# First products of experts 1 to 7 as seven products of quarters, and one buffer for each of the two weights

## The reference

```
tokens = x_flat[index].reshape(E, expert_capacity, hidden)
inter = jax.nn.relu(jnp.einsum('ech,eih->eci', tokens, first_linear))
out = jnp.einsum('eci,ehi->ech', inter, second_linear)
out = out * vals[:, :, None]
final = jnp.zeros((n_tokens, hidden), x.dtype).at[index].add(out.reshape(-1, hidden))
```

## Time and profile before

| what | before |
|---|---|
| median of three runs | 1437.44 us |
| the profiled execution itself | 1439.36 us |
| its span, first to last instruction | 1437.6 us |
| TensorE busy | 1320.3 us (92%) |
| VectorE busy | 952.7 us (66%) |
| ScalarE busy | 805.5 us (56%) |
| GpSimd busy | 739.0 us (51%) |
| TensorE in the two products, lines 1196 and 1210, share of the chain that ended last | 23% each |

### The profile page before, as it was taken

The page is one execution under the profiler, slowest core; times in us unless marked ns, Lnnn a source line. Parts: engine busy times, 40 slices in busy tenths (PEclk is TensorE's granted clock), DMA queues, the critical chain, the costliest instruction groups (busy, mean ns, idle before and its releaser), DMA issues.

```text
span 1437.6 us, 30587 instructions
## 1 busy us (share of the span) xinstructions
PE 1320.3 (92%) x12330; PEld 780.1 (54%) x12330; DVE 952.7 (66%) x1808; ACT 805.5 (56%) x1272; POOL 739.0 (51%) x781
## 2 busy tenths in 40 slices
PE   7649999989998999997849999999999999999996
PEld 3436777767676777774527444444444444444442
DVE  8768898979889787888775545454454545455421
ACT  4658888868998899987354514233241514334210
POOL 3458878877888778887323332242514224251301
PEclk9959999989999899999969999999999999999998
DMA  6157998968887786888433564565646555654401
GB/s 197 54 117 179 221 237 210 236 175 184 210 222 167 180 175 181 184 221 210 125 115 103 164 183 141 154 177 138 157 125 180 144 151 166 156 140 125 103 16 43
DMA packets 319574, 228.88 MB, mean 159 GB/s; under 512 B 253305, under 2 KB 253689, under 8 KB 319434
## 3 DMA queue, kind: packets, MB, share of 16 engines
q1 hardware_dynamic: 304074, 176.28, 49.4%
q0 software_dynamic: 15360, 50.66, 12.1%
HBM read 118.98 MB, written 50.86 MB: 118 GB/s over the span
## 4 chain that ended last, share of the span: by engine, by line
PE 74%; DVE 10%; POOL 8%; issue 3%; ACT 2%; SPq 1%; DMA 1%; DVEq 0%; POOLq 0%; ACTq 0%
PE ps L1210 23%; PE ps L1196 23%; PE ps L1096 9%; PE ps L1026 7%; PE ps L1077 3%; PE ps L1113 2%; POOL sd L547 2%; PE ps L1010 2%; DVE sm L1461 1%; PE ps L1049 1%; POOL qT L527 1%; DVE x L1483 1%; POOL ph L553 1%; PE ps L999 1%; POOL oT L533 1%
## 5 line engine op out<-in xcount | busy, mean ns | idle before, releaser
L1196 PE MATMUL ps<-xT,w1s 128*128 128x512 f16 (+1 forms) x1632 | 336.3, 368 | 1.9 <-DVE xT L1726 1.5
L1210 PE MATMUL ps<-w2s,hT 128*128 128x512 f16 x1536 | 332.8, 379 | 0.0
L848 ACT ACTIVATE hT<-ps 128x512 f16<-128x512 f32 (+1 forms) x136 | 77.5, 572 | 356.3 <-PE ps L1196 292.5
L1196 PEld LDWEIGHTS ps<-xT,w1s 128*128 128x128 f16 x1632 | 160.7, 99 | 175.3 <-issue 1.9
L1210 PEld LDWEIGHTS ps<-w2s,hT 128*128 128x128 f16 x1536 | 150.3, 98 | 181.2
L598 POOL DMA_INDIRECT out_dram<-ys,idx x64 | 71.8, 1121 | 278.0 <-DVE ys L1766 278.0
L1026 PE MATMUL ps<-xnT,wqh 128*128 128x256 f16 x1536 | 198.3, 281 | 8.2 <-ACT partq L736 8.1
L1096 PE MATMUL ps<-woh,oT 128*128 128x512 f16 x768 | 182.2, 386 | 5.4 <-POOL oT L533 5.2
L1756 DVE SCALAR_TENSOR_TENSOR hT<-ps,hT 128x512 f16<-128x512 f32 (+1 forms) x136 | 88.4, 658 | 140.4 <-ACT hT L848 88.7
L1766 DVE SCALAR_TENSOR_TENSOR ys<-ps,gs,og 128x512 f32<-128x512 f32 x64 | 48.1, 751 | 189.4 <-PE ps L1210 189.4
L553 POOL TENSOR_TENSOR ph<-sd,ph 128x1232 f16<-128x1232 f32 x64 | 162.2, 2535 | 18.7 <-ACT ph L759 18.0
(11 more groups left out here) (206 smaller groups left out, 2013.0 us busy)
## 6 DMA issues: line engine op xcount, KB each, us to landing
xr<-x SPq DMA_DIRECT2D x64, 256.0 KB, 3.4
xrow_dram<-x SPq DMA_DIRECT2D x64, 256.0 KB, 3.6
out_dram<-x SPq DMA_DIRECT2D x64, 256.0 KB, 4.0
stage<-w1T SPq DMA_DIRECT2D x8, 2048.0 KB
stage<-w2T SPq DMA_DIRECT2D x8, 2048.0 KB, 8.4
xt<-x SPq DMA_DIRECT2D x59, 256.0 KB, 3.2
xs<-x SPq DMA_DIRECT2D x56, 256.0 KB, 4.1
wqf<-wq SPq DMA_DIRECT2D x1, 1024.0 KB, 7.2
```

What stands on the lines that cost most here:

```text
L1196: ins = pe.matmul(hb[z][:, 0:wide], w1s[e % 2][:, a, k, ic * P:(ic + 1) * P], xT[:, 4 * b + k, cols], start=(k == 0 and i == 0), stop=(k = ...
L1210: ins = pe.matmul(yb[z][:, :], hT[:, a, k, s * P:(s + 1) * P], w2s[e % 2][:, b, k, :], start=(k == 0 and i == 0), stop=(k == 7 and i == 2))
```

## The change

Expert 0 stays as it was. For experts 1 to 7 the first product, a 1024 by 512 matrix of weights times 512 by 1024 of rows, is cut into four quarters on each side. By Strassen's scheme (in the form with shared sums) the four quarters of the result come from seven products of quarters (sums and differences of them) instead of eight. A quarter's product is four tiles (j = 0 to 3) of 128 by 512, each over 2 chunks in 3 passes, so 6 matmuls; 28 such tiles are 168 matmuls.

The order of the 28 tiles is the table `PRODUCTS`, pairs of product p and tile j. Products 1, 6, 7 and 4 of one j follow each other in one PSUM bank (`hb[j % 2]`); in between ScalarE copies what stands there to `running` (`part_out`), since each intermediate sum is also the start of one quarter of the result. Product 2 has bank 2, products 5 and 3 share bank 3. VectorE adds bank 2 or 3 to the copy (`sum_up`), then ScalarE makes the high part (`sum_hi`) and VectorE the low one (`sum_lo`). TensorE waits for these by the semaphores `part` and `sum`.

The sums of quarters are made by GpSimd in place: four of 128x256 for each pair of row tiles p and p + 4 (`row_sums`), four of 128x1024 for the weights (`weight_sums`). They lie between the gathers and the scatters. The split and the transpose have then 12 chunks of original rows (`raw_hi`, `raw_lo`, `raw_T`) and 16 chunks of sums (`sums_hi`, `sums_lo`, `sums_T`) for each p, and the weights have seven quarters to convert instead of four pieces of the same 1024 columns (`left_hi`, `left_lo`). `w1s` and `w2s` have one buffer each, `og` has four places instead of eight. Lines are left out where marked.

```diff
+PRODUCTS = ((1, 0), (2, 0), (5, 0), (6, 0), (1, 1), (7, 0),
+            (2, 1), (6, 1), (3, 0), (4, 0), (5, 1), (7, 1),
+            (1, 2), (2, 2), (3, 1), (6, 2), (4, 1), (5, 2), (7, 2),
+            (1, 3), (2, 3), (3, 2), (6, 3), (4, 2), (7, 3), (5, 3), (4, 3), (3, 3))
+CONVERTED = (1, 2, 4, 5, 7, 6, 3)
...
-        w1s = [sb("w1s0", [P, 2, 4, I], F16), None]
+        w1s = sb("w1s", [P, 2, 4, I], F16)
...
-        w1s[1] = sb("w1s1", [P, 2, 4, I], F16)
-        w2s = [sb(f"w2s{i}", [P, 2, 8, D], F16) for i in range(2)]
+        wq7 = sb("wq7", [P, 3, 2, 2, D], F16)
+        w2s = sb("w2s", [P, 2, 8, D], F16)
...
-        og = sb("og", [P, 8, D], F32)
+        og = sb("og", [P, 4, D], F32)
         ys = sb("ys", [P, 4, D], F32)
+        running = sb("running", [P, 3, 2, D], F32)
+        xh[1] = sb("xh1", [P, 7 * D], F16)
...
+        quarter = lambda i, j: stage1[:, :].rearrange("p (c n) -> p c n", c=4)[:, 2 * j:2 * j + 2, D * i:D * i + D]
+        left = {1: quarter(0, 0), 2: quarter(0, 1), 4: quarter(1, 1),
+                5: quarter(1, 1), 7: quarter(1, 0), 6: quarter(0, 0), 3: quarter(0, 1)}
+        left_s = {1: wq4[:, 0], 2: wq4[:, 1], 4: wq4[:, 2], 5: wq4[:, 3],
+                  6: wq7[:, 0], 7: wq7[:, 1], 3: wq7[:, 2]}
+        right_s = {1: (0, 6), 2: (2, 8), 3: (4, 10), 5: (12, 20), 4: (14, 22), 7: (16, 24), 6: (18, 26)}
...
+                if e or s >= 4:
+                    pool.wait_ge(S["y"], 8 * e + s - 3)
+                pool.indirect_dma_start(og[:, s % 4, :], None, out, rows(gix, e, s), bounds_check=N - 1,
+                                        oob_is_err=False).then_inc(S[f"g_o{s % 4}"], 16)
...
+            def row_sums(e, p):
+
+                q = 4 * (e - 1) + p
+                b11, b21 = xg[:, p, 0:256], xg[:, p, 256:512]
+                b12, b22 = xg[:, p + 4, 0:256], xg[:, p + 4, 256:512]
+                pool.wait_ge(S["xlo"], 8 + 2 * (q + 1))
+                pool.tensor_tensor(b11, b12, b11, ALU.subtract).then_inc(S["tsum"], 1)
+                pool.wait_ge(S["tsum"], 4 * q + 1)
+                pool.tensor_tensor(b12, b22, b12, ALU.subtract).then_inc(S["tsum"], 1)
+                pool.wait_ge(S["tsum"], 4 * q + 2)
+                pool.tensor_tensor(b22, b22, b11, ALU.subtract).then_inc(S["tsum"], 1)
+                pool.wait_ge(S["tsum"], 4 * q + 3)
+                pool.tensor_tensor(b21, b21, b22, ALU.subtract).then_inc(S["tsum"], 1)
+
+            def weight_sums(e):
+
+                k = 4 * (e - 1)
+                a11, a12, a21, a22 = left[1], left[2], left[7], left[4]
+                pool.wait_ge(S["w1lo"], w1_count(e, 3))
+                pool.tensor_tensor(a22, a21, a22, ALU.add).then_inc(S["wsum"], 1)
+                pool.wait_ge(S["wsum"], k + 1)
+                pool.tensor_tensor(a21, a11, a21, ALU.subtract).then_inc(S["wsum"], 1)
+                pool.wait_ge(S["wsum"], k + 2)
+                pool.tensor_tensor(a11, a22, a11, ALU.subtract).then_inc(S["wsum"], 1)
+                pool.wait_ge(S["wsum"], k + 3)
+                pool.tensor_tensor(a12, a12, a11, ALU.subtract).then_inc(S["wsum"], 1)
 
             def scatter(e, s):
...
-            for s in range(8):
-                gather_o(0, s)
             for e in range(E):
                 if e + 1 < E:
                     for s in range(8):
                         gather_x(e + 1, s)
-                if e:
-                    for s in range(8):
-                        gather_o(e, s)
+                for s in range(4):
+                    gather_o(e, s)
                 if e + 1 < E:
                     weight_max(e + 1, 1)
+                    row_sums(e + 1, 0)
+                    weight_sums(e + 1)
                 for s in range(8):
                     scatter(e, s)
+                    if s < 4:
+                        gather_o(e, s + 4)
+                    if e + 1 < E and s < 3:
+                        row_sums(e + 1, s + 1)
                 if e + 1 < E:
                     weight_max(e + 1, 2)
...
+            def left_hi(e, n):
+                p, c = CONVERTED[n], w_scale(e, 1)
+                if n == 0 and e == 1:
+                    act.wait_ge(S["f1"], f1_count(0, 15))
+                elif n == 0:
+                    act.wait_ge(S["prod"], m_count(e - 1, 3, 3))
+                if n == 0:
+                    act.wait_ge(S["w1s"], e + 1)
+                if n >= 3:
+                    act.wait_ge(S["wsum"], 4 * (e - 1) + n - 2)
...
+            def part_out(e, p, j):
+
+                n, c = {1: (1, 11), 6: (2, 12), 7: (3, 22)}[p]
+                if j >= 2:
+                    act.wait_ge(S["hlo"], h_count(e, c, j - 2))
+                act.wait_ge(S["prod"], m_count(e, p, j))
+                act.copy(running[:, n - 1, j % 2, :], hb[j % 2][:, :]).then_inc(S["part"], 1)
+
+            def sum_hi(e, c, j):
+                act.wait_ge(S["sum"], c_count(e, c, j))
+                if (c, j) == order_of[0]:
+                    act.wait_ge(S["f2"], 8 * e)
+                act.activation(h_place(0, c, j), running[:, part_of[c], j % 2, :], ACT.Relu).then_inc(S["hhi"], 1)
+
+            def last_hi(e, j):
+                act.wait_ge(S["prod"], m_count(e, 4, j))
+                act.activation(h_place(0, 21, j), hb[j % 2][:, :], ACT.Relu).then_inc(S["hhi"], 1)
 
...
+                for n, (p, j) in enumerate(PRODUCTS):
+                    if sum_of(n - 2):
+                        sum_hi(e, *sum_of(n - 2))
+                    if p in (1, 6, 7):
+                        part_out(e, p, j)
+                    if p == 4:
+                        last_hi(e, j)
+                    if p == 6:
+                        w_hi(e, 2, j)
+                sum_hi(e, 12, 3)
...
+                if p == 1 and j >= 2:
+                    pe.wait_ge(S["hlo"], h_count(e, 21, j - 2))
+                if p == 2 and j:
+                    pe.wait_ge(S["sum"], c_count(e, 11, j - 1))
+                if p == 5 and j:
+                    pe.wait_ge(S["sum"], c_count(e, 12, j - 1))
+                if p == 6:
+                    pe.wait_ge(S["part"], u_count(e, 1, j))
+                if p == 7:
+                    pe.wait_ge(S["part"], u_count(e, 6, j))
+                if p == 4:
+                    pe.wait_ge(S["part"], u_count(e, 7, j))
+                if p == 3:
+                    pe.wait_ge(S["sum"], c_count(e, 22, j))
+                fresh = p in (1, 2, 5)
+                for c in range(2):
+                    for i, (a, b) in enumerate(((0, 0), (0, 1), (1, 0))):
+                        ins = pe.matmul(bank[:, :], left_s[p][:, a, c, j * P:(j + 1) * P], xS[:, right_s[p][b] + c, :],
+                                        start=(fresh and c == 0 and i == 0), stop=(c == 1 and i == 2), skip_group_check=True)
+                ins.then_inc(S["prod"], 1)
 
             def ffn2(e, s):
...
+            def sum_up(e, c, j):
+
+                dve.wait_ge(S["part"], u_count(e, {11: 1, 12: 6, 22: 7}[c], j))
+                dve.wait_ge(S["prod"], m_count(e, {11: 2, 12: 3, 22: c22_at(j)}[c], j))
+                v = running[:, part_of[c], j % 2, :]
+                dve.tensor_tensor(v, hb[2 if c == 11 else 3][:, :], v, ALU.add).then_inc(S["sum"], 1)
...
+                y_row(e - 1, 3)
+                sums_lo(e, 2)
+                y_row(e - 1, 4)
+                sums_lo(e, 3)
+                y_row(e - 1, 5)
+                weights = weight_max(e, 2)
+                steps(weights, 2)
+                y_row(e - 1, 6)
+                steps(weights, 9)
+                gates(e)
+                y_row(e - 1, 7)
+                weights = weight_max(e + 1, 1) if e + 1 < E else iter(())
+                for n, (p, j) in enumerate(PRODUCTS):
+                    if n and PRODUCTS[n - 1][0] == 4:
+                        sum_lo(e, 21, PRODUCTS[n - 1][1])
+                    if sum_of(n):
+                        sum_up(e, *sum_of(n))
+                    if sum_of(n - 2):
+                        sum_lo(e, *sum_of(n - 2))
+                    if n == 1:
                         weight_scale(e, 2)
                         gate_scale(e)
-                    if n in (5, 7, 9, 11):
-                        w_lo(e, 2, (n - 5) // 2)
-                    if n == 14 and e + 1 < E:
-                        steps(weight_max(e + 1, 1), 9)
-                for s in range(8):
-                    if e + 1 < E:
-                        turn_x(e + 1, s)
-                        if s == 7:
-                            gates(e + 1)
```

274 lines of the change are left out of this document (199 added, 75 removed).

## The result

The changed kernel takes 1524.46 us (median of five runs, 1522.43 to 1532.42) against 1437.44 before: 1.0609 of the time, interval 1.0586 to 1.0632. It is slower, as forecast, but by 87 us and not by 26, and it lies outside the range. The profiled execution has a span of 1522.7 us, where it was 1437.6.

A forecast was written before the change was run, and what follows sets the result against it. TensorE bounds the expert half, 0.216 us a matmul. From 1439.4 us, 36.3 saved leaves 1403.1; 62.6 of new waits give 1465.7, taken as 1463; forecast case 1450 to 1476 (0.55), range 1437 to 1487.

The forecast's parts named there:

- time 0: The end of the previous expert's first product, from which the prediction counted its step times.
- The saving: First product of each of 7 experts: 24 matmuls fewer, 5.18 us an expert, 36.3 us in all.
- The change of code: GpSimd's configuration instruction ahead of the second weights' maximum, behind the last scatter: 5.9 us without computing, covered by nothing.
- the rival in which it costs nothing: GpSimd's switch between operation kinds is free once both codes are loaded, or begins early enough: 1425 us; chance 0.11.
- Single buffers: Each weight converted during the other product, when its one buffer is free: no wait beyond the preparation chain.
- the one of the transposes: SyncE's queue, first-weights load ahead of the last two transposes: last lands at 44.5 to 47, 2.4 us of wait.
- those 8.2 us: TensorE's lateness eleven tiles into a first product, VectorE's chain having waited for the second weights' maximum: 8.2 us an expert.
- The size of the sums' path: GpSimd's weight sums, then three rounds of scatter, gather and four row sums (5.85 each): last row sum ready at 37.2.
- The clock: TensorE's lower clock from pauses of about 2.4, 4 and 2 us: 0.5 us an expert, bounds 0 and 2.
- the rival with the low rate: Waits about balance the gain: row sums at low rate, GpSimd ready 1.8 us earlier, tighter VectorE steps: 1438 us; chance 0.14.

The follow-up runs named there:

- e11: e10 plus a one-column tensor operation on GpSimd behind the first weights' maximum, once for each of experts 1 to 7: 1466.6 us beside 1454.3 for the kernel before.
- e5: The change with row and weight sums made by VectorE instead of GpSimd: 1510.1 us beside 1439.9 for the kernel before.
- e10: e8 with quarters of products 6 and 3 converted behind the last sums, reductions and last low weight part moved: 1449.1 us beside 1454.3 for the kernel before.
- e2: The change with the maximum over partitions replaced by a copy for experts 1 to 7: 1538.9 us beside 1439.9 for the kernel before.
- e9: The kernel before with one buffer for each of the two weights, nothing else changed: 1438.1 us beside 1436.9 for the kernel before.
- e1: The change with each 2 MB first-weights load of experts 2 to 7 replaced by 128x16 elements: 1520.5 us beside 1439.9 for the kernel before.
- e4: The change with the next first weights' load behind the last two transposes and VectorE's reductions for it later: 1524.3 us beside 1440.3 for the kernel before.
- e3: The change with both the tiny load of e1 and the copied maximum of e2: 1511.6 us beside 1439.9 for the kernel before.
- e6: The change with sums on VectorE, the load behind the last transposes and the reductions late: 1457.3 us beside 1440.3 for the kernel before.
- e12: The change with sums on VectorE and the first-weights load of experts 2 to 7 replaced by 128x16 elements: 1448.7 us beside 1438.2 for the kernel before.
- e8: e6 with tiles needing only raw quarters first and the second weights' scale at the fifth tile: 1437.2 us beside 1436.9 for the kernel before.

## Why the prediction was wrong, step by step

All times from time 0 of expert 3, in us:

| step | predicted | measured |
|---|---|---|
| first row sum starts | 5.1 | 4.8 |
| weight sums | 10.9 to 19.7 | 11.2 to 21.7 |
| last row sum ready | 37.2 | 43.5 |
| last split done | 39.6 | 45.9 |
| last transpose there, (5,0) starts | 46.4 (at most 47) | 59.1 |
| eighth result row done | 46.6 | 55.5 |
| maximum over partitions ready | 54.5 | 63.6 |
| (5,1) starts | 62.6 | 72.4 |

**The saving** was right: 5.18 us an expert are gone from the work. **The change of code** was right in size: 42.1 us of "issue" in front of seven maxima, 5.9 to 6.2 each, and in e11 again (5.8 to 7.4). It comes with the configuration instructions: the maxima's line has 14 of them in the change and in e11 and none in the expert loop before, in e5 and in e10, where no maximum has idle time by "issue" ahead of it. It came seven times, although both kinds of operation had run before it (in the kernel before first at 1.03 and at 28.60 us), so the rival in which it costs nothing is refuted. That it is a load of code was my reading, which no run shows. What it cost the time in the change itself no run parts: e2, which takes it out, is no faster. **Single buffers** at nothing: right (e9).

**The step that failed** is the one of the transposes: "the last one now has 16 chunks, is issued at 39.7 and lands at 44.5 to 47 ... I take 2.4 us", together with "all inside those 8.2 us". Measured are 15 us late in expert 3, 93.6 us of waits in all and 17.5 us of lower clock behind them, and the wait is not inside the other but the longer of the two. Of the 12.7 us by which (5,0) comes later than I had it, 6.3 are the late sums and 6.4 the way from split to landing. Two things were wrong in it. I took the landing from single transposes of 8 chunks, although I had put 16 chunks behind a 2 MB load. And I let the issue cost nothing: in the change the last transpose stands 3.5 us in the queue and takes 6.4 to be issued, in e5 it stands 9.4. What the range of a landing was for 8 chunks was no bound for this. That an expert's transposes turn 112 chunks instead of 64 had no term in the sum at all.

**The size of the sums' path** was off as well. The last row sum came 6.3 us late: 2.0 from the weight sums (2.4 to 2.7 each, not 2.2) and 4.3 from the three rounds of scatter, gather and row sums (7.3 each, not 5.85), since a gather next to tensor operations took 1.7 to 1.95 and not 1.0 and some row sums 1.1 to 1.6. In e5, without sums on GpSimd, most gathers take 1.0 again. The eighth row lost 2.5 more to its gather, issued at 1039.61 and landed 9.7 us later into DMA engines full of transposes. From the maximum to (5,1) VectorE needed 8.8 us where I had 8.1.

**What the experiments add** is the structure. Both paths begin at the late sums on GpSimd and end at (5,1), less than 2 us apart. Taking away one at its end brings 4 us (e1), nothing (e4) or a loss (e2); both at their ends 13 (e3). Taking away the root alone brings 14, because the load then holds the transposes (e5); the root and the load 67 (e6) and 76 (e12). Only after that does the order of the tiles tell (e8). The clock was forecast at 0.5 us an expert, with 2 as the high bound, for pauses of 2 to 4 us; no run shows that 0.5, it was my estimate (the rows of before show the clock at 0.83 and 0.74 beside a pause, but no time that it cost), and what the change shows is 2.5 (17.5 us over seven experts). By the 48 matmuls from (5,0) on, 10.5 at full clock, a pause of 2.0 us cost nothing (e12), one of 4.0 cost 1.7 (e6), those of 11 to 13 us 1.4 to 2.9 (the change). A small slip in the sums changes nothing: from its own terms the rival with the low rate is 1.5 us earlier on GpSimd and not 1.8.

**Open:** what holds ScalarE's copy in e2, so that it is slower than the change and not equal, and how much of the 9 us in which a transpose lands without any load (e1) is due to the gathers and scatters beside it; no run took those away.

## What to carry to other kernels

Write the DMA queue down like an engine. For each transfer behind which TensorE waits, note what stands ahead of it in its queue, how many chunks it has, and how long its issue may be blocked, and look at which load could stand behind it without harm. Ask for the landing of the form that will be there, not of the nearest small one; where no such row exists, the high bound is open.

Where two new waits end at the same tile, neither can be priced alone. Move their common root first, and test edits in pairs: here 14 + 0 made 67.

When work goes to an engine because it has slack in sum (GpSimd had 27 us of work in 82), look at what it stands in front of: here the sums held up the scatters and gathers, these the result rows and the maximum, and those TensorE.
